# A decoder block with routed experts on one core: 32x32 block turns on VectorE in place of TensorE transposes

## What is computed

```python
# xf: 2048 rows of 512 (16 x 128 tokens); I = 352; E = 16 experts; TOP_K = 6
probs = jax.nn.softmax(xf @ gate_w.T, axis=-1)
routing_weights, selected = jax.lax.top_k(probs, TOP_K)
combine = jnp.zeros((T, E)).at[jnp.arange(T)[:, None], selected].add(routing_weights)
gate_up = jnp.einsum('th,eoh->teo', xf, w1)              # w1: 16 x 704 x 512
act = silu(gate_up[..., :I]) * gate_up[..., I:]
moe_out = jnp.einsum('te,tei,ehi->th', combine, act, w2)  # w2: 16 x 512 x 352
return moe_out + shared_out
```

## Time and profile before

| | us |
|---|---|
| runs | 1997.25, 1996.75, 1989.92 |
| median | 1996.75 |
| the profiled execution | 1988.1 |
| its span in the trace | 1985.9 |
| routed blocks: first and last copy of a down product (L1344) | 1240.2, 1980.8 |

### The profile page before, as it was taken

The page is one execution under the profiler, slowest core; times in us unless marked ns, Lnnn a source line. Parts: engine busy times, 40 slices in busy tenths (PEclk is TensorE's granted clock), DMA queues, the critical chain, the costliest instruction groups (busy, mean ns, idle before and its releaser), DMA issues.

```text
span 1985.9 us, 38759 instructions
## 1 busy us (share of the span) xinstructions
PE 1923.7 (97%) x11528; PEld 1732.7 (87%) x11529; DVE 922.6 (46%) x1974; ACT 872.9 (44%) x1991; POOL 1017.9 (51%) x1068
## 2 busy tenths in 40 slices
PE   5999999999999999999979998999999999999998
PEld 4888888888888888888868998999999999999997
DVE  4644444444565565665677364333333333333332
ACT  4654444444566575665564112333333332333332
POOL 5544444442445454444584036676433423588885
PEclk9999999999999999999989998999999999999999
DMA  9778878778888788887453347676544434599899
GB/s 333 239 255 268 266 262 264 263 254 316 289 307 288 290 309 317 294 323 285 122 195 117 96 166 246 208 246 218 176 126 126 138 120 132 153 217 212 195 215 249
DMA packets 188976, 451.56 MB, mean 227 GB/s; under 512 B 21696, under 2 KB 21952, under 8 KB 188864
## 3 DMA queue, kind: packets, MB, share of 16 engines
q1 hardware_dynamic: 135392, 339.89, 50.7%
q0 software_dynamic: 21504, 51.13, 10.9%
q10 hardware_dynamic: 31968, 59.12, 9.3%
HBM read 276.13 MB, written 173.92 MB: 227 GB/s over the span
## 4 chain that ended last, share of the span: by engine, by line
PE 86%; DMA 4%; DVE 3%; issue 2%; POOL 2%; ACT 2%; SPq 1%; ACTq 0%; POOLq 0%; DVEq 0%
PE bank L1128 21%; PE bank L986 15%; PE bank L1138 12%; PE bank L1033 8%; PE bank L1010 7%; PE bank L167 6%; PE bank L581 5%; DMA xT<-xT_att 4%; PE bank L591 3%; PE bank L1019 2%; PE bank L1041 2%; PE bank L598 2%; PE bank L1052 1%; SPq L875 1%; DVE qS L529 0%
## 5 line engine op out<-in xcount | busy, mean ns | idle before, releaser
L1128 PE MATMUL bank<-w_hi,xT 128*128 x1776 | 473.9, 329 | 2.1 <-DVE xT L1703 2.1
L986 PE MATMUL bank<-w_hi,xT 128*128 128x512 f32 x1024 | 355.6, 408 | 11.8 <-DMA xT<-xT_att 9.8
L1128 PEld LDWEIGHTS bank<-w_hi,xT 128*128 128x128 f32 x1776 | 316.1, 189 | 9.3 <-issue 4.2
L1404 POOL TENSOR_TENSOR rr<-rr,expo 128x4 f32<-128x4 f32 x128 | 129.1, 1008 | 345.9 <-DVE rr L1599 345.5
L608 DVE TENSOR_TENSOR hT<-bank,hT 128x384 fp32r<-128x384 f32 x143 | 79.7, 557 | 472.2 <-ACT hT L605 472.2
L1128 PE MATMUL bank<-w_lo,xT 128*128 x888 | 286.5, 323 | 0.0
L986 PEld LDWEIGHTS bank<-w_hi,xT 128*128 128x128 f32 x1024 | 194.0, 189 | 56.5 <-issue 10.5
L1138 PE MATMUL bank<-w_hi,hT 128*128 x666 | 229.9, 399 | 2.9 <-DVE hT L608 2.4
L605 ACT ACTIVATE hT<-bank 128x384 fp32r<-128x384 f32 x143 | 70.2, 491 | 319.4 <-PE bank L598 300.0
L1010 PE MATMUL bank<-w_hi,xT 128*128 128x256 f32 x1024 | 208.7, 289 | 0.0
L986 PE MATMUL bank<-w_lo,xT 128*128 128x512 f32 x512 | 203.3, 397 | 0.0
(11 more groups left out here) (238 smaller groups left out, 4128.4 us busy)
## 6 DMA issues: line engine op xcount, KB each, us to landing
xT<-xT_att SPq DMA_DIRECT2D x126, 512.0 KB, 5.3
w_hi<-w_split SPq DMA_DIRECT2D x64, 512.0 KB, 6.9
w_lo<-w_split SPq DMA_DIRECT2D x64, 512.0 KB, 7.9
xg<-blank SPq DMA_DIRECT2D x111, 264.0 KB, 5.0
yg<-blank SPq DMA_DIRECT2D x111, 256.0 KB, 5.8
raw<-in_weights SPq DMA_DIRECT2D x82, 276.0 KB, 3.3
w_split<-w_hi SPq DMA_DIRECT2D x64, 276.0 KB, 3.5
w_split<-w_lo SPq DMA_DIRECT2D x64, 276.0 KB, 3.9
```

What stands on the lines that cost most here:

```text
L986: last = pe.matmul(bank[par][:, :], xT[:, par, a, c * P:(c + 1) * P], w_hl[w][:, fw, c * 512:(c + 1) * 512], start=n == 0, stop=n == 11)
L1128: last = pe.matmul(out_[:, 0:I], xT[:, par, a, c * P:(c + 1) * P], flat(w_hl[w])[:, bass.ds(at + (c * CW + half_ * (I + E)), I)], start=n ...
L1404: pool.tensor_tensor(rr[:, :], rr[:, :], expo[:, :], ALU.pow).then_inc(pw_done, 1)
```

## The change

PE's seven transposes of a block go. In the place of the four on rows, ACT loads the rows by five DMAs: four that put 32x32 blocks where a transposed matrix has them, in pieces of 512 bytes, and one for the 16 shares, in pieces of 64 bytes; then one VectorE instruction turns the 32x32 blocks (`turn`). In the place of the three on hidden values, `hidden` writes to one of two buffers, ACT stores these to memory in pieces of 384 bytes (`hidden_store`), loads them back with blocks exchanged (`hidden_load`), and VectorE turns the blocks (`turn_hidden`). The host orders weights to match. The down product comes two blocks behind gate and up, loads run three blocks ahead and stand after the block's copies, the value loads for weights and shares move to VectorE, and POOL's third scatter is made before it prepares the second expert's weights, the fourth and fifth right after these, the sixth after the third expert's (before, the third to sixth came after the weights of the second to fifth expert).

```diff
 # PE
-                def block_step(i, par, front, nxt, load, back, last_at=None):
+                def block_step(i, par, front, back):
                     if front:
...
                         first_at(par, at, 0, GATE[par], g_done)
-                    if back:
-                        pe.wait_ge(hid_done, NSH + i)
-                        hidden_transposes(pe, HT_)
-                    if nxt:
-                        pe.wait_ge(x_in[1 - par], 8 * (i + 1 - (1 - par)) + 16)
-                        transposed(1 - par, trS)
-                    if front:
                         first_at(par, at, 1, UP[par], u_done)
                     if back:
-                        second_at(last_at, YF[1 - par])
+                        before = columns(i - 2)
+                        pe.wait_ge(hT_hi, NSH + i - 1)
+                        pe.wait_ge(hT_lo, NSH + i - 1)
+                        second_at(before, YF[par])
 # ACT
                 def load(i, par, rounds_):
                     act.wait_ge(rounds, rounds_)
-                    act.dma_start(xin[par], xg[bass.ds(i * P, P), :]).then_inc(x_in[par], 16)
+                    rows = xg[bass.ds(i * P, P), :]
+                    for a in range(NQUAD):
+                        act.dma_start(xin[par][a * QUAD:(a + 1) * QUAD, 0:D].rearrange("t (q c) -> t q c", q=NQUAD),
+                                      rows[:, a * P:(a + 1) * P].rearrange("(q t) c -> t q c", q=NQUAD))\
+                            .then_inc(x_in[par], 16)
+                    act.dma_start(xin[par][:, D:DW], rows[:, D:DW]).then_inc(x_in[par], 16)
+                def hidden_store(i, par):
+                    act.wait_ge(hid_done, NSH + i + 1)
+                    act.dma_start(hid_rows[par].rearrange("a r c -> r a c"),
+                                  hidb[par].rearrange("p (a c) -> p a c", a=NQUAD)).then_inc(h_st[par], 16)
+                def hidden_load(i, par):
+                    act.wait_ge(h_st[par], 8 * (i - par) + (H_ST + 16))
+                    act.dma_start(hidq[par], hid_rows[par].rearrange("a (t q) c -> (a t) (q c)", q=NQUAD))\
+                        .then_inc(h_in[par], 16)
 # POOL
-                for k in range(2):
+                for k in range(TOPK // 2):
                     scatter(k)
...
-                    if 2 <= e + 1 < TOPK:
-                        scatter(e + 1)
+                    if e == 1:
+                        scatter(3)
+                    if e + 3 < TOPK:
+                        scatter(e + 3)
 # DVE
+                def turn(i, par):
+                    dve.wait_ge(x_in[par], LOADS * 8 * (i - par) + LOADS * 16)
+                    dve.transpose(TX_[:, :], xin[par][:, 0:D].rearrange("p (q k c) -> p k q c", q=NQUAD, k=KC))\
+                        .then_inc(trS, 1)
...
+                def turn_hidden(i, par):
+                    dve.wait_ge(h_in[par], 8 * (i - par) + (H_IN + 16))
+                    dve.wait_ge(hT_lo, NSH + i)
+                    dve.transpose(HT_[:, 0:IP].rearrange("p (k t q) -> p k q t", k=IC, q=NQUAD),
+                                  hidq[par].rearrange("p (q k c) -> p k q c", q=NQUAD, k=IC)).then_inc(ht_done, 1)
...
+                    if nxt:
+                        need = turn(i + 1, 1 - par)
+                        dve.wait_ge(w_ready, need)
                         dve.wait_ge(xs_hi, i + 2)
                         split_lo(1 - par)
+                    if back:
+                        turn_hidden(i - 2, par)
+                        dve.wait_ge(hT_hi, NSH + i - 1)
+                        hidden_lo(dve, HT_)
```

More of the change, by code:

```diff
@@ L776, in rec_slots @@
             return [SPLIT + 2 * t, SPLIT + 2 * t + 1] if t < ROUTE_AT else [None] * 2
[L778 to L790, removed]
+        ROUNDS_BY = 3 * B + 10
         ROUTE_AT = 20
@@ L1179, in _ @@
+                pe.wait_ge(hid_done, NSH + NBLK + NQUAD - 1)
+                for c in range(IC):
+                    last = pe.transpose(TX_[:, c * P:(c + 1) * P], hidb[0][:, c * P:(c + 1) * P], ident[:, :])
+                last.then_inc(ht_last, 1)
+                block_step(NBLK, 1, False, True)
+                before = columns(NBLK - 1)
+                pe.wait_ge(hT_hi, NSH + NBLK)
+                pe.wait_ge(hT_lo, NSH + NBLK)
+                second_at(before, YF[0], hT_last)
             @block.scalar
@@ L1321, in block_step @@
+                def block_step(i, par, front, nxt, ahead, first_, back):
                     if nxt:
-                        need = weights_for(i + 1)
-                    if back:
-                        act.wait_ge(ht_done, NSH + i)
-                        hidden_hi(act, HT_)
+                        act.wait_ge(trS, i + 2)
+                        act.wait_ge(u_done, NSH + i)
+                        split_hi(1 - par)
                     if front:
@@ L1370, in _ @@
+                block_step(NBLK - 1, 0, True, False, None, False, True)
+                act.wait_ge(ht_done, NSH + NBLK - 1)
+                act.wait_ge(yF_done, NSH + NBLK - 2)
+                hidden_hi(act, HT_)
+                act.wait_ge(ht_last, 2)
+                act.activation(hT_last[:, 0, :], TX_[:, 0:IP], ACT.Copy).then_inc(hT_hi, 1)
+                y_store(NBLK - 2, 1)
+                y_store(NBLK - 1, 0)
             @block.gpsimd
@@ L1750 @@
         downs.append(sw2[:, h * I:(h + 1) * I])
[L1751 removed]
+    by_quad = np.arange(D).reshape(NQUAD, KC, QUAD).transpose(1, 0, 2).reshape(-1)
+    ups += [a["L0_ffn_w1"][e][:, by_quad] for e in range(E)]
     downs += [a["L0_ffn_w2"][e] for e in range(E)]
[L1753 removed]
+    hid_by_quad = np.arange(IP).reshape(NQUAD, IC, QUAD).transpose(1, 0, 2).reshape(-1)
+    for n, (up, down) in enumerate(zip(ups, downs)):
         w2 = np.concatenate([down.T, np.zeros((IP - I, D), np.float32)], axis=0)
+        w2 = w2 if n < 2 else w2[hid_by_quad]
         logits = a["L0_ffn_gate_w"] if len(groups) == NG else np.zeros((E, D), np.float32)
```

166 lines of the change are left out of this document (95 added, 71 removed).

## The result

| | us |
|---|---|
| changed kernel, median of four runs (2140.81 to 2150.56) | 2146.23 |
| kernel before, beside it (1989.92 to 1997.25) | 1996.24 |
| ratio, with its 95% interval | 1.0768 (1.0744 to 1.0791) |
| span of the profiled execution, after and before | 2148.4, 1985.9 |

What follows compares the result with a forecast made beforehand. PE, busy 97% of the span, was taken to bound the kernel, with gathers the largest loss after the change: 1988.1 - 7 + 14 + 104 + 2 = 2101, put at 2105 us toward the runs' median; range 1970 to 2165.

Steps and rivals of the forecast that it cites:

- the range: Whole kernel: 1970 to 2165 us, meant to hold in 8 of 10 cases.
- its own range: Whole kernel: the forecast's own case, an end between 2050 and 2165 us, chance 0.52.
- the gathers: Last 39 blocks: packets shared one for one with POOL's queue, 17.6 us a block while a gather runs, 104 us lost.
- the sum: Whole kernel: 1988.1 - 7 + 14 + 104 + 2 = 2101 us, with 17.6 us a block in a gather.
- ACT's sequencer: Blocks before 72: seven issues take 3.29 us, its sequence 6.34, or 6.64 with a value load; 7 us gained.
- PE's part: Each block: 0.69 us of transposes go, a 6.46 us loop through ACT and DVE leaves 0.24 gained, 0.45 waiting before down.
- POOL's order: Early blocks: with scatters moved ahead, block 12 waits for the third expert's weights until 1322; 14 us lost.
- The lower bound: Blocks in a gather: ACT waits for a landing of 6.3 us and makes six issues, 9.1 us from store to store.
- Faster: Rival for the whole kernel: PE stays the bound, loop about 6.1 us, POOL sets the end, 1954 us; chance 0.17.
- The mild case: Rival for blocks in a gather: small packets are cheap, 9.1 us a block holds, 2040 us in all; chance 0.17.
- Dear small stores: Rival for all blocks: 384-byte stores cost 171 ns a piece, 8.5 us a block even in quiet, about 2230; chance 0.08.
- The signs: PE's share falls; wait behind hidden_lo 0.3 to 0.6 us; copies 6.4 to 6.7 apart in quiet, over 12 in gathers.

Runs made afterwards that it cites:

- a_no_gather: The changed kernel with five of its six gathers left out, so that only one runs, at the end; 2089.75 us.
- k_no_trip: The changed kernel with hidden loads reading a second array, so that they wait for no store, same transfers; 2116.93 us, ratio 1.0626.
- f2_rows_only: The kernel before with rows turned by VectorE, loaded three blocks ahead, hidden values still transposed by PE; 1951.99 us, ratio 0.9806.
- e_hid_plain: The changed kernel with hidden values stored plainly, 128 pieces of 1536 bytes instead of 512 of 384; 2126.21 us.
- g_hid_only: The changed kernel with rows loaded by one DMA and transposed by PE, hidden values still by way of memory; 2173.23 us, ratio 1.0917.

## Why the prediction was right, and where its steps were not

The direction, the range and its own range (2050 to 2165) held, and the mechanism in part: PE stopped being the bound, and the gathers cost the most, but by the latency that the sum had put aside. Two terms were off in opposite ways, ACT's sequencer by 70 us too little loss and the gathers by 30 too much, and the start, 18 us later, stood in no term. That the total came as near as 41 us is partly luck.

**PE's part** was right in kind: PE stopped being the bound, the transposes' time became a wait before down, in just the chain that was written out. Its size wasn't: 6.46 was forecast, 6.84 and 7.3 in turn came. The rows of after tell the terms: down to the copy 2.40 instead of 2.28; 0.48 from the issue of the store to `split_hi` instead of 0.36; and 0.25 from the end of `hidden_lo` (1751.86) to the down product, where 0.04 had been put, a hop that the rows before didn't isolate. The turn was right, 0.58 for 0.56. The branch of the loop, some 0.45 in every second block, was left out: before, it lay beside PE's work, and it had cost nothing. The Trainium skill's price for a turn ("VectorE: DVE Perf Modes", The three transpose paths), 311 ns for 128x128 in bf16, would have given 0.93 for the three, an estimate; the trace, in fp32, has 0.58 for the three, and 0.73 for the rows' four.

**ACT's sequencer** is the first term that failed: "7 us gained" before block 72 became 72.3 - 9.4 (the wait for weights) = 63 lost. The seven issues were well sized, 1754.26 - 1750.86 = 3.40 for 3.29; the value load in the first 58 blocks costs 0.63, not 0.30, and the branch comes on top. (At 0.36 an issue the loop of 6.46 would have been the bound, and the gain 72 x 0.24 = 17 us, not the 20 of the prediction.) Two loops of 6.46 and 6.34 were put down as a gain of 0.24, when half a us more in the longer one makes a loss of the same size; fed by the same steps, they should have had a wider bound in the sum.

**POOL's order**: 14 forecast; the gap of 17.2 us is 9.4 over its neighbours. The weights came at 1333.5, 12 us later than worked out, but blocks were late by then too.

**The gathers** are the second term that failed: 104 forecast, 74 measured. Of these 49 are five gathers' (a_no_gather), 18 the last one's, with the output beside it, and 13 the quiet pace; the last three blocks give 6 back. The step was the choice of 17.6 us a block, "since the packets were counted where both queues were loaded". ACT's queue wasn't full there: from 1832 to 1862, before, it moved 1188 packets beside 2000, about what blocks of 6.66 us ask for at 256 packets each, 1150, and PE had no gap. So the ratio was what it asked for, not what it could get: it got nearly two for one after. The lower bound, from store landing to store landing, 9.1, was the mechanism: 10.55 in the trace, 7.5 until the store had landed plus three us of issues. That this loop is a latency is shown by the half with PE's hidden transposes (no loss, at nearly as many packets a microsecond) and, for half of it, by k_no_trip; that something at the queue follows behind it, by k_no_trip's held issues.

**The rivals.** Faster did not come, but its bound did in f2_rows_only: PE sets the pace, 6.31 us a block, and POOL's last gather (from 1905.47) ends with PE. Its 1952 us are near the 1954 of that rival by luck: the rival had a shorter block and a wait for weights. The mild case had nearly the right price of a block in a gather, 9.1 against 8.6 to 10.5 in the first, and lost to the quiet. Dear small stores are refuted by the quiet pace, 7.1 where they would have made it 8.5, and by e_hid_plain, where their size makes no difference. The Trainium skill's rule ("DMA: Bandwidth & Descriptors", Specifications), that under 512 bytes the engines read, modify and write, may explain the 11 us in the last 39 blocks; no run here tells that from the smaller number of packets.

**The signs.** PE's lower share and a wait behind hidden_lo came, the wait a little longer (0.57 us, and 1.0 to 1.24 with the branch, for 0.3 to 0.6). The distances of the copies did not: 6.83 to 7.9 us in the quiet for 6.4 to 6.7, and in the first gather 8.6 to 10.5 for over 12.

## What to carry to other kernels

When a busy engine is relieved, its wait is set by the order in which the other engines do their work, so before counting what is saved write down the loop from its last product back to its next, and ask which of the steps in it belong to other blocks; here moving two steps ahead of two others was worth 81 us. A way through memory costs two landings in a row, and its distance in blocks has to be set by the worst moment of the program (here 6.3 and 5.5 us), not by the quiet one (2.2 and 2.6); that more distance would have mended it was not tried. And a change with two halves is worth trying as two: one of these alone was a gain of 2%, the other hid it.

## What the runs showed of the hardware that had not been expected

- VectorE's turn of 32x32 blocks takes as long as another operation on the same values: 0.73 us for 128x512, 0.58 for 128x384 (L1728, L1738), against 0.69 and 0.56 for the splits.
- A DMA issue on ACT's sequencer, 0.33 to 0.48 us in quiet stretches, took up to 3.79 us beside a gather, in k_no_trip.
- Two queues on the same DMA engines didn't share packet for packet: in a gather 4369 packets of ACT's, most of them under 2 KB, went beside 2271 of POOL's in 30 us, and in k_no_trip 5863 beside 1729.
- Matmuls of the down product started 0.43 us apart instead of 0.23 in four of the blocks 12 to 56, where PE had waited 1.9 to 2.2 us before them; another wait of 1.9 us, ahead of 1687.51, was not followed by this. The granted clock was 0.97 from 1640 to 1700 and 0.89 in the gather from 1832 to 1862, means between its levels of 1.2 and 2.4 GHz. In g_hid_only, where PE waited some 1.4 us in every block, it was 1.00 from 1700 to 1800.
